# Three stacked graph-attention layers on one core: the extremes read two count tiles later, and first maxima two ahead on two accumulators

## The chip, the core and the metric

One NeuronCore of a Trainium2 chip runs the whole program. The metric is the device time of one execution in microseconds. The engines are named as in the profile: PE is TensorE, PEld its weight loads, DVE VectorE, ACT ScalarE, POOL GpSimd, and SP the engine that issues most of the DMAs.

## The reference

`x` has 3125 nodes of 128 features, and 103125 edges `src -> dst` are sorted by `dst`. Three attention layers run in two residual blocks:

```python
h = jnp.maximum(_layernorm(x, axis=-1), 0.0)
x = x + _L0_gnn_ref(h, ...)     # two layers, 128 -> 256 -> 128 features
h = jnp.maximum(_layernorm(x, axis=-1), 0.0)
x = x + _L1_gnn_ref(h, ...)     # one layer, 128 -> 128

def gat_layer(x, src, dst, W, a_src, a_dst, b, n_nodes):
    h = x @ W
    s, d = h @ a_src, h @ a_dst
    e = leaky_relu(s[src] + d[dst], 0.2)
    ex = exp(e - segment_max(e, dst)[dst])
    alpha = ex / segment_sum(ex, dst)[dst]
    return segment_sum(alpha[:, None] * h[src], dst) + b
```

(Each layer adds one loop per node to the edges. `edge_feat` is computed and never used.)

## The kernel before

**Dense form.** The edges are turned once into a table of counts `C`, kept in SBUF as 8-bit floats: for each pair of nodes, how many edges join them. Each layer then works on the dense 3125 x 3125 matrix. It is cut into 15 chunks `q` (3 layers x 5 chunks of 625 destinations), and each chunk into 25 source tiles `s` of 125 sources. I call the layers 0, 1, 2; chunks 0 to 4, 5 to 9 and 10 to 14 are theirs. Chunks 5 and 10 open a layer ("turn").

**Count stage.** 40 count tiles `t`. For each, VectorE makes two one-hot planes (L951), TensorE multiplies them (L1780), ScalarE copies the counts to `C` (L1452). Between the tiles other work is placed by tile number: after tile `EXT_AT` VectorE takes each partition's extremes of the attention terms (L968 to L980). SP writes them to DRAM and reads them back spread over all partitions. After tile `OVER_AT` VectorE reduces what came back (L997) and makes some scalars, and at tile `EXPS_AT` ScalarE makes exponentials from them. Then a row `g` goes through DRAM, and GpSimd makes the blocks of chunk 0 (L743, L751). TensorE multiplies these during count tiles `EARLY_AT` to 35.

**A chunk.** For a source tile `s`, `slot[s]` receives a block of 125 x 625 weights. It is either made by VectorE alone in one operation (`product`, L1149, from a row of exponentials that TensorE spreads over the partitions in PSUM) or by ScalarE (L1567, L1569) and GpSimd (L751) together. TensorE multiplies it by the features: 5 matmuls (L1813) a tile, in order of `s`, the last two tiles by L1821. Eight slots go round as a ring. I write P0, P1, P10, P24 for VectorE's product of tile 0, 1, 10, 24. Layer 1 has VectorE products at 0, 1, 2, 4, 8, 10, 14, 16, 20, 24, layer 2 the same without 0, and a turn chunk at 0, 1, 2, 4, 6, 8, 10, 12, 14, 16, 18, 24.

**First maxima.** Before the sums of chunk `q` can be scaled, the largest term of each destination is needed. VectorE runs 25 steps k0 to k24 over it (`next_top`, `top_step`, L1067; a first step of an accumulator is L1069), joins two accumulators `TOP0` and `TOP1` in PSUM (L1073), and TensorE transposes the result early in the next chunk (L1789), where VectorE reduces it (L1079, "the reduction" below). A step on an accumulator waits for the last step on the same one. The steps of chunk `q` stand between the products of chunk `q` at the places that `top_at(q, k)` gives. The first `AHEAD` of them come at the end of the chunk ahead, after its P24, and by `in_odd` all of these use `TOP0`:

```python
            return k >= AHEAD and k % 2 == 1     # in_odd: the step is on TOP1
```

**The rows.** TensorE spreads the row for chunk `q + 1` (`fast_rows`, L1803) after its tile 22 of chunk `q` (23 in a turn chunk), into the PSUM that the products of chunk `q` read. So it waits for P24 of chunk `q`, and nothing of chunk `q + 1` that reads it can start earlier:

```python
                dve.wait_ge(F.rows_ready, q)       # in product(q, s), and at s == 0 if that tile is GpSimd's
                pe.wait_ge(prod_done, prod_no(q, 0))   # in fast_rows(q)
```

The order on every engine is written out in the code; each engine runs its list in order, and semaphores join them.

Of the kernel before, what the change touches and what calls it, by code (L numbers as in the profile page):

```python
# [7 lines left out]
def gat_stack_kernel(nc, x, edges, apart, W1, a_src1, a_dst1, b1, W2, a_src2, a_dst2, b2,  # L8
# [11 lines left out]
    T = N // P  # L20
# [46 lines left out]
    with ctx:  # L67
# [290 lines left out]

        LAYERS = 3
        Q = LAYERS * NC  # L360
        AHEAD = 5
        PASS_AHEAD = 6
        EARLY_TILES = 15
        LATE = 20
# [2 lines left out]

        KEYS_TILE = 4
        FEAT_AT = tuple(KEYS_TILE + 2 + r for r in range(len(FEATS)))
        EXT_AT = FEAT_AT[-1] + 2  # L370
        OVER_AT = EXT_AT + 1
        EXPS_AT = OVER_AT + 1
        SECOND = 0
        EARLY_AT, EARLY_TO = EXPS_AT + 4, NT - 4
# [38 lines left out]
        def turn(q):  # L413
            return q and q % NC == 0

        def spread_tops(q, k0, k1, s0, s1):
            return tuple((s0 + (k - k0) * (s1 - s0) // (k1 - k0), q, k) for k in range(k0, k1))

        AFTER = T
        FIRST_TOPS = (None,  # L420
                      spread_tops(0, AHEAD, T, 0, 13) + spread_tops(1, 0, 10, 14, 25) + spread_tops(1, 10, 14, AFTER, AFTER),
                      spread_tops(1, 14, T, 0, 10) + spread_tops(2, 0, 17, 10, 25) + spread_tops(2, 17, 21, AFTER, AFTER),
                      spread_tops(2, 21, T, 0, 4) + spread_tops(3, 0, T, 4, 24) + spread_tops(4, 0, AHEAD, AFTER, AFTER))

# [18 lines left out]
        def in_odd(k, q=None):  # L443
            if q in (1, 2):
                return k % 2 == 1 and not any(at_ == AFTER and (c, k) == (q, k_) for at_, c, k_ in FIRST_TOPS[q])
            return k >= AHEAD and k % 2 == 1

# [8 lines left out]
        def top_at(q, k):  # L456
            if turn(q) and k >= LATE:
                return (21, 21, 22, 22, 23)[k - LATE]
            return (k - AHEAD) * (T - 3) // (T - 1 - AHEAD)

        def join_at(q):
            return top_at(q, T - 1) if turn(q) else top_at(q, T - 1) + 1
# [407 lines left out]
        def _(dve):  # L870
# [69 lines left out]
            def one_hots(t, part=None):  # L940
                c, i = t // JT, t % 2
                first, last_w = SPLIT[t % JT], SPLIT[t % JT + 1]
                w0, w1_ = 0, last_w - first
                if part is not None:
                    w0, w1_ = HALF[part][0], min(HALF[part][1], w1_)
                if t > 1 and w0 == 0:
                    dve.wait_ge(half_ok[1], t - 1)
                for n, (hot, key, m) in enumerate(((hot_lo[i], key_lo, COLS), (hot_col[i], key_col, P))):
                    if t % JT == 0:
                        dve.wait_ge(keys_sb, 2 * c + n + 1)  # L950
                    last = v.tensor_tensor(hot[:, w0:w1_, :, :],  # L951
                                           key[:, c, first + w0:first + w1_, :].unsqueeze(2).broadcast_to(
                                               [128, w1_ - w0, m, LANES]),
                                           iota_ps[:, 0:m, :].unsqueeze(1).broadcast_to([128, w1_ - w0, m, LANES]),
                                           ALU.is_equal)
                last.then_inc(hots_ok, 1)
# [14 lines left out]
            def extremes_early(L):  # L971
                if L:
                    dve.wait_ge(F.new_sb, (L - 1) * NC + EARLY_TILES // CT)
                    dve.wait_ge(ext_out, 16 * (2 * L - 1))
                else:
                    dve.wait_ge(ab_ready, len(FEATS))
                t1 = EARLY_TILES if L else T
                extremes(L, 0, t1)
                dve.wait_ge(ext_lin, EXT_NO[L])
                v.tensor_reduce(ext[:, 1:2], a_neg[:, 0:t1], AX.X, ALU.max).then_inc(ext_ready, 1)  # L980
# [14 lines left out]
            def over_nodes(e, into, done):  # L995
                dve.wait_ge(ext_in, 16 * (e + 1))
                v.tensor_reduce(into[:, :], ext_rows.rearrange("p (n i) -> p i n", i=2), AX.X, ALU.max).then_inc(done, 1)  # L997
# [44 lines left out]
            for t in range(KEYS_TILE + 1, NT - 1):  # L1042
                one_hots(t)
                if t == EXT_AT:
                    extremes_early(0)
                if t == OVER_AT:
                    over_nodes(0, extg[0], extg_ready)
# [105 lines left out]
            def next_top(q, k):  # L1153
                L = q // NC
                if turn(q) and k in (0, EARLY_TILES, LATE):
                    dve.wait_ge(unit_ready, 3 * L - 1 + (0, EARLY_TILES, LATE).index(k))
                top_step(F, a_unit[L % 2], q, k)
# [8 lines left out]
            def chunk(q):  # L1166
                L, c = q // NC, q % NC
                for s in range(T):
# [4 lines left out]
                    if q < len(FIRST_TOPS):  # L1173
                        first_tops(q, s)
                    else:
                        for k in range(AHEAD, T):
                            if top_at(q, k) == s:
                                next_top(q, k)
                        if s == join_at(q):
                            join_tops(F, q)  # L1180
# [33 lines left out]
                elif q < Q - 1:  # L1214
                    for k in range(AHEAD):
                        next_top(q + 1, k)
# [826 lines left out]
```

## Time and profile before

| | us |
|---|---|
| median of 3 runs | 687.71 (687.67 to 689.26) |
| the profiled execution | 687.7 |
| its span, first to last instruction | 686.0 |
| VectorE busy | 639.8 (93%) |
| TensorE busy | 587.9 (86%) |
| ScalarE busy | 484.7 (71%) |
| GpSimd busy | 459.6 (67%) |

The span is 1.7 us shorter than the execution's own time. A busy share is an average over the count stage (to about 204 us) and the chunks.

### The profile page before, as it was taken

The page shows a single profiled execution, that of the slowest core. Times are in us where ns is not written, and L with a number is a line of the kernel's source. Part 1 is how long each engine was busy: PE and PEld are TensorE (multiplying, and loading weights), DVE is VectorE, ACT ScalarE, POOL GpSimd, SP SyncE. Part 2 cuts the span into 40 slices and gives each one's busy share as a digit, 9 for nine tenths or more (in the row PEclk, how much of TensorE's full clock was granted, in tenths as well). Part 3 has the DMA queues.
Part 4 walks back from the last instruction along what each step waited for, and adds up shares of the span by engine and source line. Part 5 has one row for each costly group of instructions (what it writes and reads, how often), then busy time and mean ns, then how long its engine had stood idle before and what let it go on. Part 6 is the DMA issues. An engine that isn't in the chain of part 4 may idle for free.

```text
span 686.0 us, 13824 instructions
## 1 busy us (share of the span) xinstructions
PE 587.9 (86%) x5571; PEld 570.1 (83%) x5571; DVE 639.8 (93%) x911; ACT 484.7 (71%) x719; POOL 459.6 (67%) x448
## 2 busy tenths in 40 slices
PE   1728845989869899999999979999989989999995
PEld 1628744988769899989999979899989979999994
DVE  3999979999999989999987999999998899999994
ACT  0416543655969787887765878989886698898891
POOL 5579103589908656675954775858598688697883
PEclk9959977899999899999999999999999999999998
DMA  2410002000000000000100100000010010110001
GB/s 69 119 56 2 1 9 38 1 2 1 20 1 1 20 1 20 1 1 9 20 20 1 27 1 20 1 19 2 8 20 20 1 27 3 37 29 11 20 1 42
DMA packets 22325, 12.07 MB, mean 18 GB/s; under 512 B 12393, under 2 KB 20055, under 8 KB 22255
## 3 DMA queue, kind: packets, MB, share of 16 engines
q1 hardware_dynamic: 21455, 9.85, 6.2%
q0 software_dynamic: 800, 1.26, 0.6%
q8 instruction: 46, 0.75, 0.5%
q14 instruction: 24, 0.20, 0.1%
HBM read 9.47 MB, written 1.64 MB: 16 GB/s over the span
## 4 chain that ended last, share of the span: by engine, by line
DVE 52%; PE 28%; issue 8%; DMA 6%; POOL 4%; ACT 1%; POOLq 0%; DVEq 0%; SPq 0%
PE ps L1813 21%; DVE scratch L951 21%; DVE ps L1067 16%; DVE scratch L1149 5%; DMA xr<-in_x 3%; POOL scratch L751 2%; DVE ps L1069 2%; DVE ps L1079 1%; PE ps L1866 1%; PE ps L1821 1%; DMA gathered<-ext_lines 1%; PE ps L1844 1%; DVE scratch L1067 1%; DMA gathered<-in_edges,start_i 1%; DMA ext_lines<-ext 1%
## 5 line engine op out<-in xcount | busy, mean ns | idle before, releaser
L1813 PE MATMUL ps<-hB,scratch 125*125 125x129 f32 x3450 | 404.7, 276 | 21.3 <-DVE scratch L1149 17.8
L1813 PEld LDWEIGHTS ps<-hB,scratch 125*125 125x125 f32 x3450 | 390.7, 189 | 28.6 <-DVE scratch L1149 23.0
L751 POOL TENSOR_TENSOR scratch<-scratch,C 125x625 f32<-125x625 f32 x239 | 304.1, 1283 | 124.1 <-ACT scratch L1569 122.1
L1067 DVE SCALAR_TENSOR_TENSOR ps<-C,a_unit,ps 125x625 f32<-125x625 fp8e3 x330 | 275.5, 867 | 2.3
L1567 ACT ACTIVATE scratch<-gathered,r_neg 125x625 f32<-125x625 f32 x219 | 176.6, 806 | 18.7 <-PE ps L1813 17.5
L1569 ACT ACTIVATE scratch<-scratch,r_src 125x625 f32<-125x625 f32 x219 | 179.0, 817 | 7.1
L1452 ACT ACTIVATE C<-ps 125x1000 fp8e3<-125x1000 f32 x80 | 78.0, 1000 | 78.5 <-PE ps L1780 78.3
L1780 PE MATMUL ps<-scratch 128*128 128x125 bf16 x1250 | 90.3, 235 | 40.0 <-DVE scratch L951 38.1
L1780 PEld LDWEIGHTS ps<-scratch 128*128 128x128 bf16 x1250 | 83.0, 105 | 46.8 <-DVE scratch L951 44.7
L1149 DVE SCALAR_TENSOR_TENSOR scratch<-ps,r_src,C 125x625 f32<-125x625 f32 x121 | 104.2, 861 | 4.2 <-PE ps L1803 4.1
L951 DVE TENSOR_TENSOR scratch<-key_lo,ps 128x4096 bf16<-128x4096 bf16 (+3 forms) x41 | 89.8, 2190 | 0.0
L951 DVE TENSOR_TENSOR scratch<-key_col,ps 128x4000 bf16<-128x4000 bf16 (+3 forms) x41 | 87.9, 2144 | 0.0
L1069 DVE TENSOR_SCALAR ps<-C,a_unit 125x625 f32<-125x625 fp8e3 x30 | 25.8, 865 | 0.2
L756 POOL TENSOR_TENSOR scratch<-scratch,rz 125x640 f32<-125x640 f32 x14 | 17.6, 1258 | 11.8 <-DVE rz L1126 11.8
L743 POOL TENSOR_SCALAR scratch<-gathered,r_src 125x625 f32<-125x625 f32 x20 | 15.7, 783 | 10.7 <-DMA gathered<-g_lines 10.7
L1550 ACT ACTIVATE kappa<-back 125x5 f32<-125x5 f32 x15 | 3.1, 207 | 27.0 <-DVE back L1093 26.9
L1821 PE MATMUL ps<-hB,scratch 125*125 125x129 f32 x150 | 21.6, 274 | 0.0
L1821 PE MATMUL ps<-hB,gathered 125*125 125x129 f32 x150 | 21.4, 273 | 0.0
L728 POOL TENSOR_TENSOR shift<-sigma,tau 125x1 f32<-125x1 f32 x3 | 0.6, 192 | 30.7 <-DVE tau L1013 30.7
L1079 DVE TENSOR_REDUCE ps<-ps 125x5 f32<-125x625 f32 x15 | 12.2, 812 | 8.2 <-PE ps L1789 8.2
L790 POOL TENSOR_TENSOR hB<-hA,e_src 125x645 f32<-125x645 f32 x15 | 19.0, 1265 | 0.0
L1821 PEld LDWEIGHTS ps<-hB,scratch 125*125 125x125 f32 x150 | 18.8, 187 | 0.2 <-POOL scratch L751 0.2
(195 smaller groups left out, 451.5 us busy)
## 6 DMA issues: line engine op xcount, KB each, us to landing
gathered<-g_lines SPq DMA_DIRECT2D x15, 305.2 KB
xr<-in_x SPq DMA_DIRECT2D x1, 1562.5 KB
out<-xr SPq DMA_DIRECT2D x4, 312.5 KB
edge_sb<-in_edges SPq DMA_DIRECT2D x1, 805.7 KB
gathered<-ext_lines SPq DMA_DIRECT2D x5, 122.1 KB
w<-in_W SPq DMA_DIRECT2D x2, 128.0 KB
out<-xr SPq DMA_DIRECT2D x1, 187.5 KB
out<-xr SPq DMA_DIRECT2D x1, 125.0 KB
```

The source lines that it names most:

```text
L751: g.tensor_tensor(slot[s], slot[s], C5[:, q % NC, s, :], ALU.mult).then_inc(pool_done, 1)
L951: last = v.tensor_tensor(hot[:, w0:w1_, :, :], key[:, c, first + w0:first + w1_, :].unsqueeze(2).broadcast_to([128, w1_ - w0, m, LANES]), ...
L1067: v.scalar_tensor_tensor(dest, counts, unit[:, s:s + 1], top, ALU.min, ALU.max).then_inc(S.top_done, 1)
L1069: v.tensor_scalar(dest, counts, unit[:, s:s + 1], None, ALU.min).then_inc(S.top_done, 1)
L1079: v.tensor_reduce(mu[:, :], tiles(WORK), AX.X, ALU.max).then_inc(S.top_max, 1)
L1149: v.scalar_tensor_tensor(slot[s].rearrange("p (t n) -> p t n", n=P), tiles(ROWU), r_src[L % 2][:, s:s + 1], C5[:, c, s, :].rearrange("p (t ...
L1452: a_.activation(C5[:, c, :, rows].rearrange("p t (w q) -> p t w q", q=WQ), tiles(place(t, i), w1_ - w0).rearrange("p w (t q) -> p t w q", ...
L1567: a_.activation(A, ga[q % 2], ACT.Relu, bias=r_neg[L % 2][:, s:s + 1]).then_inc(over_done, 1)
L1569: a_.activation(A, A, ACT.Identity, bias=r_src[L % 2][:, s:s + 1]).then_inc(rowmax_ok, 1)
L1780: last = mm(ps[0:128, o:o + WC], hot_lo[i][:, w, :, k], hot_col[i][:, w, :, k], start=(k == 0), stop=(k == KC - 1))
L1813: last = mm(ps[0:P, acc_at(t):acc_at(t) + HW], A[:, P * t:P * (t + 1)], feat, start=opens and t in (0, 3), stop=closes, skip_group_check=True)
L1821: last = mm(ps[0:P, acc_at(t):acc_at(t) + HW], slot[s][:, P * t:P * (t + 1)], hB3[:, s, :], start=False, stop=s == T - 1, skip_group_check ...
```

## The change

Three constants and one formula. `AHEAD` falls from 5 to 2; `top_at` spreads the other 23 steps over places 0 to 21, where 20 steps stood at 0 to 22; `EXT_AT` goes from 14 to 15 and `OVER_AT` from 15 to 17. `EXPS_AT` (16 to 18) and `EARLY_AT` (20 to 22) follow from `OVER_AT`.

```diff
-        AHEAD = 5
+        AHEAD = 2
@@
-        EXT_AT = FEAT_AT[-1] + 2
-        OVER_AT = EXT_AT + 1
+        EXT_AT = FEAT_AT[-1] + 3
+        OVER_AT = EXT_AT + 2
         EXPS_AT = OVER_AT + 1
         SECOND = 0
         EARLY_AT, EARLY_TO = EXPS_AT + 4, NT - 4
@@
-            return (k - AHEAD) * (T - 3) // (T - 1 - AHEAD)
+            return (k - AHEAD) * (T - 4) // (T - 1 - AHEAD)
```

Worked out (T is 25): before, k5 to k24 stand at places 0, 1, 2, 3, 4, 5, 6, 8, 9, 10, 11, 12, 13, 15, 16, 17, 18, 19, 20, 22. Now k2 and k3 stand at 0, then k4 at 1, k5 at 2, and so on to k23 at 20 and k24 at 21. The work of no engine changes in amount.

The first place is VectorE in the count stage, around the extremes (L968 to L980) and what is read back (L997). The rows with + and - are those that moved.

```order
 L951 TENSOR_TENSOR scratch<-key_col,ps 128x4000
+L951 TENSOR_TENSOR scratch<-key_lo,ps 128x3328
+L951 TENSOR_TENSOR scratch<-key_col,ps 128x3250
 L968 TENSOR_SCALAR a_neg<-ab 125x25
 L969 TENSOR_REDUCE ext<-ab 125x1
 L980 TENSOR_REDUCE ext<-a_neg 125x1
-L951 TENSOR_TENSOR scratch<-key_lo,ps 128x3328
-L951 TENSOR_TENSOR scratch<-key_col,ps 128x3250
+L951 TENSOR_TENSOR scratch<-key_lo,ps 128x4096
+L951 TENSOR_TENSOR scratch<-key_col,ps 128x4000
+L951 TENSOR_TENSOR scratch<-key_lo,ps 128x4096
+L951 TENSOR_TENSOR scratch<-key_col,ps 128x4000
 L997 TENSOR_REDUCE extg<-gathered 125x2
```

One count tile (two L951) stood between the extremes and the reading back, and now there are two, both full ones.

The second place is VectorE at the border of chunks 6 and 7 (layer 1), from P24 to the reduction L1079 of the chunk ahead. Before:

```order
L1149 SCALAR_TENSOR_TENSOR gathered<-ps,r_src,C 125x625
L1069 TENSOR_SCALAR ps<-C,a_unit 125x625
L1067 SCALAR_TENSOR_TENSOR ps<-C,a_unit,ps 125x625 x4
L1149 SCALAR_TENSOR_TENSOR scratch<-ps,r_src,C 125x625
L1069 TENSOR_SCALAR ps<-C,a_unit 125x625
L1149 SCALAR_TENSOR_TENSOR scratch<-ps,r_src,C 125x625
L1067 SCALAR_TENSOR_TENSOR ps<-C,a_unit,ps 125x625
L1149 SCALAR_TENSOR_TENSOR scratch<-ps,r_src,C 125x625
L1067 SCALAR_TENSOR_TENSOR ps<-C,a_unit,ps 125x625
L1079 TENSOR_REDUCE ps<-ps 125x5
```

Now, at the same border:

```order
L1149 SCALAR_TENSOR_TENSOR gathered<-ps,r_src,C 125x625
L1069 TENSOR_SCALAR ps<-C,a_unit 125x625
L1067 SCALAR_TENSOR_TENSOR ps<-C,a_unit,ps 125x625
L1149 SCALAR_TENSOR_TENSOR scratch<-ps,r_src,C 125x625
L1067 SCALAR_TENSOR_TENSOR ps<-C,a_unit,ps 125x625
L1069 TENSOR_SCALAR ps<-C,a_unit 125x625
L1149 SCALAR_TENSOR_TENSOR scratch<-ps,r_src,C 125x625
L1067 SCALAR_TENSOR_TENSOR ps<-C,a_unit,ps 125x625
L1149 SCALAR_TENSOR_TENSOR scratch<-ps,r_src,C 125x625
L1067 SCALAR_TENSOR_TENSOR ps<-C,a_unit,ps 125x625
L1079 TENSOR_REDUCE ps<-ps 125x5
```

P24 and P0 (the first two L1149) have two steps between them in place of five; between P0 and the reduction there are four steps in place of three.

The third place is VectorE at the border of chunks 11 and 12 (layer 2, where tile 0 is GpSimd's), from P24 to P1. Before:

```order
L1149 SCALAR_TENSOR_TENSOR gathered<-ps,r_src,C 125x625
L1069 TENSOR_SCALAR ps<-C,a_unit 125x625
L1067 SCALAR_TENSOR_TENSOR ps<-C,a_unit,ps 125x625 x4
L1069 TENSOR_SCALAR ps<-C,a_unit 125x625
L1149 SCALAR_TENSOR_TENSOR scratch<-ps,r_src,C 125x625
```

Now:

```order
L1149 SCALAR_TENSOR_TENSOR gathered<-ps,r_src,C 125x625
L1069 TENSOR_SCALAR ps<-C,a_unit 125x625
L1067 SCALAR_TENSOR_TENSOR ps<-C,a_unit,ps 125x625 x2
L1069 TENSOR_SCALAR ps<-C,a_unit 125x625
L1149 SCALAR_TENSOR_TENSOR scratch<-ps,r_src,C 125x625
```

Four steps stand between P24 and P1 in place of six. The wait for the rows (at `s == 0`) stood before the sixth step; it now stands before the third.

## Rows read from the trace of the kernel before

**Rows 1.** Busy time in a stretch of layer 2, each engine's us and count

```profile
583.00:612.00 29.00, 28.82 (x261) 28.61 (x261) 28.79 (x45) 25.51 (x36) 23.41 (x19) 1.00 0.08 23
```

**Rows 2.** VectorE in order of time, count stage: start us, us, operation, idle before

```profile
92.71 0.18 DVE L980 TENSOR_REDUCE ext<-a_neg 125x1 f32<-125x25 f32 x1
...
99.83 0.41 DVE L997 TENSOR_REDUCE extg<-gathered 125x2 f32<-125x250 f32 x1 [3.39 <-DMA gathered<-ext_lines]
...
101.15 2.28 DVE L951 TENSOR_TENSOR scratch<-key_lo,ps 128x4096 bf16<-128x4096 bf16 x1
...
105.50 2.28 DVE L951 TENSOR_TENSOR scratch<-key_lo,ps 128x4096 bf16<-128x4096 bf16 x1
```

**Rows 3.** ScalarE in order of time, count stage

```profile
101.27 0.32 ACT L1476 ACTIVATE g_row<-b_cut,sigma 125x25 f32<-125x25 f32 x1 [2.01 <-DVE tau L1013]
```

**Rows 4.** GpSimd in order of time, first and last block of chunk 0

```profile
114.85 0.79 POOL L743 TENSOR_SCALAR scratch<-gathered,r_src 125x625 f32<-125x625 f32 x1 [10.74 <-DMA gathered<-g_lines]
...
178.23 1.31 POOL L751 TENSOR_TENSOR gathered<-gathered,C 125x625 f32<-125x625 f32 x1
```

**Rows 5.** TensorE in order of time, where chunk 0 ends

```profile
188.56 0.87 PE L1821 MATMUL ps<-hB,scratch 125*125 125x129 f32 x6
```

**Rows 6.** VectorE in order of time, chunks 6 to 7, layer 1

```profile
416.51 0.87 DVE L1149 SCALAR_TENSOR_TENSOR gathered<-ps,r_src,C 125x625 f32<-125x625 f32 x1
...
418.19 3.60 DVE L1067 SCALAR_TENSOR_TENSOR ps<-C,a_unit,ps 125x625 f32<-125x625 fp8e3 x4
421.82 0.87 DVE L1149 SCALAR_TENSOR_TENSOR scratch<-ps,r_src,C 125x625 f32<-125x625 f32 x1
...
426.79 0.82 DVE L1079 TENSOR_REDUCE ps<-ps 125x5 f32<-125x625 f32 x1 [0.22 <-PE ps L1789]
...
436.40 0.84 DVE L1149 SCALAR_TENSOR_TENSOR scratch<-ps,r_src,C 125x625 f32<-125x625 f32 x1
437.15 3.19 DVE L1067 SCALAR_TENSOR_TENSOR ps<-C,a_unit,ps 125x625 f32<-125x625 fp8e3 x4
```

**Rows 7.** TensorE in order of time, chunks 6 to 7

```profile
421.01 0.71 PE L1803 MATMUL ps<-ident,g_row 125*125 125x125 f32 x5
...
429.86 6.87 PE L1813 MATMUL ps<-hB,scratch 125*125 125x129 f32 x60 [0.90 <-DVE scratch L1149]
437.29 6.87 PE L1813 MATMUL ps<-hB,scratch 125*125 125x129 f32 x60 [0.56 <-DVE scratch L1149]
...
453.36 0.71 PE L1803 MATMUL ps<-ident,g_row 125*125 125x125 f32 x5
```

**Rows 8.** TensorE in order of time, chunks 5, 9 and 10

```profile
361.55 2.47 PE L1813 MATMUL ps<-hB,scratch 125*125 125x129 f32 x20 [0.50 <-DVE scratch L1149]
...
509.60 1.36 PE L1813 MATMUL ps<-hB,scratch 125*125 125x129 f32 x10 [0.92 <-POOL scratch L751]
...
537.65 4.80 PE L1813 MATMUL ps<-hB,scratch 125*125 125x129 f32 x40 [0.64 <-DVE scratch L1149]
```

**Rows 9.** VectorE in order of time, P0 of chunk 5

```profile
350.21 0.87 DVE L1149 SCALAR_TENSOR_TENSOR scratch<-ps,r_src,C 125x625 f32<-125x625 f32 x1 [2.57 <-PE ps L1803]
```

**Rows 10.** P0 of chunk 6 on VectorE

```profile
387.33 0.87 DVE L1149 SCALAR_TENSOR_TENSOR scratch<-ps,r_src,C 125x625 f32<-125x625 f32 x1
```

**Rows 11.** TensorE's rows for chunk 6

```profile
385.37 0.71 PE L1803 MATMUL ps<-ident,g_row 125*125 125x125 f32 x5
```

**Rows 12.** TensorE in order of time, chunks 11 and 12, layer 2

```profile
565.66 19.54 PE L1813 MATMUL ps<-hB,scratch 125*125 125x129 f32 x175 [0.72 <-DVE scratch L1149]
...
586.68 0.71 PE L1803 MATMUL ps<-ident,g_row 125*125 125x125 f32 x5
...
594.82 21.19 PE L1813 MATMUL ps<-hB,scratch 125*125 125x129 f32 x190 [0.18 <-DVE scratch L1149]
```

**Rows 13.** VectorE in order of time, the sixth step (k5) of chunk 12

```profile
588.54 0.87 DVE L1069 TENSOR_SCALAR ps<-C,a_unit 125x625 f32<-125x625 fp8e3 x1
```

**Rows 14.** Who waited for whom, whole span: us in total, times, longest

```profile
PE ps L1813 <- DVE scratch L1149: 17.8, 24, 3.6
DVE scratch L1149 <- PE ps L1803: 4.1, 2, 2.6
```

## The prediction

> **What bounds the kernel now.** I read the table of waits first, then the engines side by side in order of time. The waits [rows 14] show TensorE and VectorE waiting for each other: TensorE 17.8 us in 24 places for products, VectorE 4.1 us in 2 places for the spread rows. Neither is the bound alone: in layer 2 both are busy for 28.8 of 29 us [rows 1]. The count stage is VectorE's: its one-hots stand end to end, 4.35 us a full tile (105.50 less 101.15), and it stops once, 3.39 us, for the extremes that come back through DRAM [rows 2].
>
> In the chunks the order of time shows a loop. Take chunk 7, layer 1. TensorE spreads the rows at 421.01 and is done at 421.72. P0 starts at 421.82, 0.10 later [rows 6, 7]. The four steps ahead of it start at 418.19 and end at 421.79, so their starts are 0.91 apart, and the next operation could have started at about 421.7 [rows 6]. So P0 waits for the rows, just barely, and the five steps ahead are what fills the time. From P0 VectorE runs to P10 (436.40, done 437.24); TensorE waits for P10 (0.56 us) and starts at 437.29. From there it has no wait until the next rows at 453.36 [rows 6, 7]. The loop is rows, P0, P10, TensorE, rows: 453.36 - 421.01 = 32.35 us. What stands between P0 and P10 costs its time in every turn of it. What stands between P24 and P0 costs nothing, as long as it ends before the rows do. Chunk 5 shows that more plainly: its P0 waits 2.57 us for the rows [rows 9].
>
> **The change part by part.**
>
> *The extremes.* They were done at 92.89 and their reduction could start at 99.83, so the trip takes 6.9 us [rows 2]. Now two full tiles, 8.7 us, lie over it: the wait of 3.39 is gone, with 1.8 us to spare. What is late next is the start of chunk 0's blocks. The scalars come two tiles less 3.39 later, 5.3 us, and ScalarE now has to empty count tile 17 before its exponentials, which it did not have to wait for at 101.27 [rows 3]; I put `g` 7 us later, at most 8.7. GpSimd then starts at about 122 in place of 114.85. Its last block was done at 179.54 and TensorE took it at 188.56, 9.0 us later [rows 4, 5]; TensorE now comes 3.4 earlier, and 9.0 - 3.4 = 5.6 is less than 7. But GpSimd stood idle for ScalarE's four blocks in that stretch, and this idle time shrinks when it starts late, since they stay tied to count tiles. I take it as hidden. If not, it costs up to 8.7 - 5.6 = 3.1 us. **-3.4 us.**
>
> *The alternation.* Steps on one accumulator start 0.91 us apart, alternating ones (3.19 - 0.87) / 3 = 0.77 apart [rows 6]. So each step that no longer follows one on its own accumulator saves 0.13 us. That counts only where VectorE is not waiting behind it: at the start of chunk 1, where k0 to k24 stand in one run and TensorE waits for their end, it is 2 x 0.13. **-0.3 us.** The Trainium skill ("VectorE: DVE Perf Modes", section "The DRAIN you can't avoid") says that the next operation doesn't start until the pipe is empty, and that a semaphore between them costs nothing. By that both spacings would be equal and this term zero, the sum 0.3 higher; the rows show 0.77 against 0.91, and I go by them.
>
> *Layer 1, chunks 7 and 8.* Between P24 and P0 there are now 2 steps. VectorE is ready for P0 at about 419.1 and waits 2.7 us for the rows, which are no earlier. From P0 to P10 (places 0 to 9) stood k5 to k13, 9 steps; now k2 to k12, 11 steps. Two more at 0.77 are 1.55. The reduction between them waited 0.22 us for TensorE's transposes [rows 6], which one more step ahead of it swallows: +1.3. TensorE's wait for P10 goes from 0.56 to about 1.3 (and that for P4, 0.90 now, to 1.4 [rows 7]); nothing behind P10 has room to give it back, since TensorE then runs without a wait. P14 has the same two steps more and P16 to P24 three, but TensorE takes 1.1 us a tile (6.87 us for six [rows 7]) and comes to them later and later. **+2.6 us for both.** Bounds: 0 (if VectorE's lead were kept) and 2 x 1.55 = 3.1.
>
> *Layer 1, the others.* Chunk 6: P0 was not held by the rows; it started at 387.33, the rows were done at 386.08 [rows 10, 11]. Now it can start at 386.18, 1.15 earlier, and P10 comes 1.55 - 1.15 = 0.4 later, or 0.6 with a wait at the reduction. **+0.6.** Chunk 9: P10 is 1.5 late, but TensorE then waits 0.92 us for GpSimd's tile 15 [rows 8], whose work hangs on VectorE's scalars at place 4, one step late. **+0.8.**
>
> *The turns.* Chunk 5: P0 is held by the rows before and after [rows 9]. The last wait of TensorE for VectorE is at 361.55, for P6 [rows 8]: k2 to k8 stand ahead of it in place of k5 to k10, one more. **+0.8.** Chunk 10: the last one is at 537.65, for P10 [rows 8], with 11 steps in place of 9. **+1.55.** Chunk 4 opens in the same way but TensorE is behind VectorE there; between 0 and one step, I take **+0.2.** Chunks 0 to 3 keep their order but for single steps.
>
> *Layer 2.* The wait for the rows now stands ahead of k2. The rows of chunk 12 are done at 587.39 and k5 started at 588.54 [rows 12, 13], 1.05 after it could have. Now k2 starts at 587.5, k3 0.77 later, P1 at 589.0 where it was 588.54 + 0.77 = 589.3. So the first products are 0.3 earlier here, P10 and P14 one step (0.77) later than they, and TensorE's wait of 0.18 for P4 goes [rows 12]. At P10 it comes back in part. In chunk 11 a wait of 0.72 shrinks in the same way. Bounds: 0 and 0.72 + 3 x 0.18 = 1.3 gained. The low end is nearer, as P10 takes over. **-0.4 us.**
>
> The sum: -3.4 - 0.3 + 2.6 + 0.6 + 0.8 + 0.8 + 1.55 + 0.2 - 0.4 = +2.45 us. The profiled execution took 687.7 us, its span 686.0, and the median of the runs is 687.71, so the same sum holds for both: **690.1 us**.
>
> **The rivals.**
>
> *Half of it.* Somewhere the extra steps meet time that VectorE or TensorE would have waited anyway: the 0.22 wait at the reduction is one such place, and the 0.92 wait for GpSimd another. If each loop lost only one step (0.77) in chunks 5 to 10, they would cost 4.6 in place of 6.35, and with the gain of layer 2 at its upper end the time is 687.7 - 3.7 + 4.6 + 0.2 - 1.3 = 687.5; with one of the two, 688.2. For it: VectorE's list holds many small operations that wait for their own results. Against it: P0 starts 0.10 us after the rows, as close as a release can follow.
>
> *Faster: the loop is not held at the rows.* The mechanism is that P0 can come earlier with two steps ahead than with five. If TensorE reaches its tile 22 earlier than now, because P4 and P10 were its only waits, then P0 moves up and VectorE's 0.1 us a step of alternation adds up. That needs the rows at least 1.3 us earlier a chunk in layer 1; from there on nothing is lost, and the time is 687.7 - 3.7 = 684.0, less with layer 2. For it: in chunk 6 P0 does move up by 1.15 us. Against it: the rows come after tile 22 in TensorE's list, and TensorE works without a pause from 437.29 to 453.36 [rows 7].
>
> *Slower still.* VectorE's steps at place 3 also feed the factor that ScalarE needs before its further blocks, and these go to GpSimd and on to TensorE. If ScalarE's chain is then the later one, the loops lose 1.55 each where I take 0.6 to 0.8, in chunks 5, 6 and 9 (+2.5), or GpSimd comes late in the count stage (+3.1): about 692.5.
>
> **How the numbers follow.** The forecast as worked out 0.52, half of it 0.23, faster 0.13, slower still 0.12. The forecast's own range is 689.0 to 691.2. For eight in ten I leave out the faster case and part of the slowest: 686.9 to 692.2. A run here can tell about 0.3% (2.06 us) from no change, so the borders are 685.65 and 689.77. The forecast lies above the upper one, but close: of its 0.52 I put 0.33 above and 0.19 inside; half of it falls inside; so slower 0.45, same 0.42, faster 0.13.
>
> **What the profile after would show.** L997 in the count stage without an idle time, and what follows it 3.4 us earlier. VectorE waiting 2 to 3 us for L1803 ahead of each P0 of chunks 4 to 10, several times the 4.1 that stand now [rows 14], and TensorE's waits for L1149 near 1.3 us at P4 and P10. Rows of layer 1 33.65 us apart in place of 32.35; layer 2 chunks at 29.0 to 29.1. If P0 in layer 1 has no wait, the loop is not what I say. If the rows are 32.3 us apart although P0 waits, TensorE's wait at P10 was not on it. If TensorE waits for GpSimd in the 130 to 190 us of the count stage, the first term is too good.

## The result, and the profile after

| | before | after |
|---|---|---|
| median, us | 687.71 (687.63 to 689.26, 5 runs) | 691.26 (690.71 to 691.95, 5 runs) |
| span of the profiled execution | 686.0 | 689.3 |

The ratio is 1.0047, with a 95% interval of 1.0033 to 1.0062: the changed kernel is slower by 3.5 us. The forecast was 690.1 us, range 686.9 to 692.2; 691.26 lies 0.06 us outside the narrow range of the forecast as worked out (689.0 to 691.2).

The count stage first. VectorE in order of time (start us, us, operation, idle before in brackets), the rows that answer to [rows 2]:

```profile
96.10 0.18 DVE L980 TENSOR_REDUCE ext<-a_neg 125x1 f32<-125x25 f32 x1
...
104.88 0.41 DVE L997 TENSOR_REDUCE extg<-gathered 125x2 f32<-125x250 f32 x1
```

L997 has no idle time left. ScalarE's `g`, GpSimd's first and last block of chunk 0, and TensorE at the end of chunk 0, which answer to [rows 3 to 5]:

```profile
108.52 0.30 ACT L1476 ACTIVATE g_row<-b_cut,sigma 125x25 f32<-125x25 f32 x1
...
121.66 0.79 POOL L743 TENSOR_SCALAR scratch<-gathered,r_src 125x625 f32<-125x625 f32 x1 [11.03 <-DMA gathered<-g_lines]
...
178.92 1.31 POOL L751 TENSOR_TENSOR gathered<-gathered,C 125x625 f32<-125x625 f32 x1
...
184.91 0.87 PE L1821 MATMUL ps<-hB,scratch 125*125 125x129 f32 x6
```

`g` is 7.25 us later (108.52 less 101.27) and GpSimd starts 6.8 later, but its last block is only 0.7 later and TensorE still takes it 3.65 us earlier than before. So GpSimd's idle time swallowed the delay.

The loop of layer 1, chunks 6 to 7, VectorE from P24 to P10 and TensorE from rows to rows (answering to [rows 6, 7]):

```profile
412.55 0.87 DVE L1149 SCALAR_TENSOR_TENSOR gathered<-ps,r_src,C 125x625 f32<-125x625 f32 x1
413.33 0.86 DVE L1069 TENSOR_SCALAR ps<-C,a_unit 125x625 f32<-125x625 fp8e3 x1
414.23 0.87 DVE L1067 SCALAR_TENSOR_TENSOR ps<-C,a_unit,ps 125x625 f32<-125x625 fp8e3 x1
417.56 0.87 DVE L1149 SCALAR_TENSOR_TENSOR scratch<-ps,r_src,C 125x625 f32<-125x625 f32 x1 [2.46 <-PE ps L1803]
...
422.99 0.81 DVE L1079 TENSOR_REDUCE ps<-ps 125x5 f32<-125x625 f32 x1
...
433.37 0.84 DVE L1149 SCALAR_TENSOR_TENSOR scratch<-ps,r_src,C 125x625 f32<-125x625 f32 x1
```

```profile
416.74 0.71 PE L1803 MATMUL ps<-ident,g_row 125*125 125x125 f32 x5
...
426.05 6.93 PE L1813 MATMUL ps<-hB,scratch 125*125 125x129 f32 x60 [1.13 <-DVE scratch L1149]
434.26 6.87 PE L1813 MATMUL ps<-hB,scratch 125*125 125x129 f32 x60 [1.29 <-DVE scratch L1149]
...
450.33 0.71 PE L1803 MATMUL ps<-ident,g_row 125*125 125x125 f32 x5
```

P0 waits 2.46 us for the rows, from P0 to P10 it is 15.81 us where it was 14.58, the reduction has lost its wait, and the rows are 33.59 us apart (450.33 less 416.74) where they were 32.35. In chunk 5, P0 waits 3.48 us ([rows 9]: 2.57); in chunk 6 it now waits too, 1.48 us, where it was not held ([rows 10, 11]).

TensorE's waits in chunk 5 and chunk 10 (answering to [rows 8]), and both engines in layer 2 ([rows 12, 13]):

```profile
357.47 2.47 PE L1813 MATMUL ps<-hB,scratch 125*125 125x129 f32 x20 [0.50 <-DVE scratch L1149]
...
538.16 2.03 PE L1813 MATMUL ps<-hB,scratch 125*125 125x129 f32 x16 [1.29 <-DVE scratch L1149]
...
587.59 0.71 PE L1803 MATMUL ps<-ident,g_row 125*125 125x125 f32 x5
...
602.98 14.58 PE L1813 MATMUL ps<-hB,scratch 125*125 125x129 f32 x130 [0.72 <-DVE scratch L1149]
```

```profile
588.33 0.87 DVE L1067 SCALAR_TENSOR_TENSOR ps<-C,a_unit,ps 125x625 f32<-125x625 fp8e3 x1 [0.19 <-PE ps L1803]
```

In layer 2, k2 does start right after the rows, as forecast, but TensorE now waits 0.72 us for P10, where it had no wait for it. And the table of waits, whole span (us in total, times, longest; [rows 14]), with the busy times from 583 to 612 us, same columns as [rows 1]:

```profile
PE ps L1813 <- DVE scratch L1149: 22.6, 23, 2.5
...
DVE scratch L1149 <- PE ps L1803: 15.5, 7, 3.5
```

```profile
583.00:612.00 29.00, 28.28 (x255) 28.03 (x254) 28.70 (x44) 25.16 (x35) 22.78 (x19) 1.00 0.08 24
```

TensorE is busy 0.54 us less in the same 29 us: that is the new wait.

**Where the 3.3 us of the span lie.** I compare the starts of the rows L1803 of each chunk. "Chunk 7" is the time from the rows for chunk 7 to the rows for chunk 8. Chunk 0 lies in the first line; chunks 2 and 3 differ by 0.01 and are left out.

| part | before | after | difference | forecast |
|---|---|---|---|---|
| to the rows for chunk 1 | 204.24 | 200.60 | -3.64 | -3.4 |
| chunk 1 | 34.02 | 32.71 | -1.31 | -0.3 |
| chunk 4 | 35.02 | 35.11 | +0.09 | +0.2 |
| chunk 5 | 36.00 | 36.77 | +0.77 | +0.8 |
| chunk 6 | 35.64 | 35.46 | -0.18 | +0.6 |
| chunks 7, 8 | 64.69 | 67.17 | +2.48 | +2.6 |
| chunk 9 | 34.46 | 35.20 | +0.74 | +0.8 |
| chunk 10 | 35.64 | 37.19 | +1.55 | +1.55 |
| chunks 11 to 14, to the end | 130.20 | 133.00 | +2.80 | -0.4 |

One pair of profiles carries these differences, and the same program varies between profiled executions: in the nine profiles with the changed kernel's count stage the rows for chunk 1 stand at 200.60 to 203.72 us, and the changed kernel's own is the earliest of them. So the first line may not be read to 0.1 us; the times of whole runs below carry it.

Three lines are off: chunk 1, chunk 6 and layer 2. The experiments go after these, and after the loop itself.

### The profile page after: what moved, and what is told of

It reads as the page before. It is cut to its first block, busy times and chain, and to the rows that moved or that the text cites. A ratio compares the mean times of both kernels' runs of the same rounds, so it can differ in the third digit from the quotient of the medians.

```text
span 689.3 us, 13825 instructions
## 1 busy us (share of the span) xinstructions
PE 593.0 (86%) x5571; PEld 573.9 (83%) x5571; DVE 639.6 (93%) x911; ACT 485.8 (70%) x719; POOL 459.6 (67%) x448
## 4 chain that ended last, share of the span: by engine, by line
DVE 43%; PE 37%; issue 8%; DMA 5%; POOL 4%; ACT 2%; POOLq 0%; DVEq 0%
PE ps L1813 29%; DVE scratch L951 20%; DVE ps L1067 10%; DVE scratch L1149 5%; DMA xr<-in_x 3%; POOL scratch L751 2%; PE ps L1866 2%; DVE ps L1079 1%; PE ps L1844 1%; PE ps L1803 1%; PE ps L1836 1%; PE ps L1869 1%; DMA gathered<-in_edges,start_i 1%; ACT scratch L1567 1%; PE ps L1780 1%
## 5 line engine op out<-in xcount | busy, mean ns | idle before, releaser
L1780 PE MATMUL ps<-scratch 128*128 128x125 bf16 x1250 | 93.3, 239 | 32.7 <-DVE scratch L951 30.8
L1780 PEld LDWEIGHTS ps<-scratch 128*128 128x128 bf16 x1250 | 85.7, 108 | 40.0 <-DVE scratch L951 37.9
L1149 DVE SCALAR_TENSOR_TENSOR scratch<-ps,r_src,C 125x625 f32<-125x625 f32 x121 | 104.2, 861 | 15.5 <-PE ps L1803 15.5
L951 DVE TENSOR_TENSOR scratch<-key_lo,ps 128x4096 bf16<-128x4096 bf16 (+3 forms) x41 | 89.3, 2179 | 0.0
L951 DVE TENSOR_TENSOR scratch<-key_col,ps 128x4000 bf16<-128x4000 bf16 (+3 forms) x41 | 87.4, 2132 | 0.0
L756 POOL TENSOR_TENSOR scratch<-scratch,rz 125x640 f32<-125x640 f32 x14 | 17.6, 1257 | 16.7 <-DVE rz L1126 16.7
L1821 PEld LDWEIGHTS ps<-hB,gathered 125*125 125x125 f32 x150 | 18.8, 188 | 0.0
```

The costliest lines, as they stand in the source:

```text
L951: last = v.tensor_tensor(hot[:, w0:w1_, :, :], key[:, c, first + w0:first + w1_, :].unsqueeze(2).broadcast_to([128, w1_ - w0, m, LANES]), ...
L1149: v.scalar_tensor_tensor(slot[s].rearrange("p (t n) -> p t n", n=P), tiles(ROWU), r_src[L % 2][:, s:s + 1], C5[:, c, s, :].rearrange("p (t ...
L1780: last = mm(ps[0:128, o:o + WC], hot_lo[i][:, w, :, k], hot_col[i][:, w, :, k], start=(k == 0), stop=(k == KC - 1))
L1821: last = mm(ps[0:P, acc_at(t):acc_at(t) + HW], slot[s][:, P * t:P * (t + 1)], hB3[:, s, :], start=False, stop=s == T - 1, skip_group_check ...
```

## The experiments

My theory of the loss was the loop of the prediction: a step between P0 and P10 costs its time in every turn. The rival to it: what is lost is the lead of three steps over a chunk's border, wherever they are put. For layer 2 the theory at hand was the extra step, or a collision with GpSimd (below). Each run has the kernel before beside it on the same chip; the ratio is to that.

### The two halves apart

```diff
 # e1_extremes_only: before, with
+        EXT_AT = FEAT_AT[-1] + 3
+        OVER_AT = EXT_AT + 2
 # e2_two_ahead_only: before, with
+        AHEAD = 2
+            return (k - AHEAD) * (T - 4) // (T - 1 - AHEAD)
```

> The kernel before with the extremes' part alone (EXT_AT 15, OVER_AT 17); AHEAD stays 5. My theory: the chunks keep their periods of before, and all is earlier by what the count stage gained, 3.6 us at chunk 1's first maxima: 684.1 us. Whether the further 1.3 us that chunk 1 gained in the changed kernel comes with this part (its ScalarE and GpSimd work is placed by count tile) is open: then 682.8 us. Rival: the gain is given back where later work waits for something that did not move; then 686 us or more.

> The kernel before with AHEAD 2 and the new top_at alone; the extremes stay where they were. If the two parts add up, 691.3 + 3.6 = 694.9 us, or 691.3 + 5.0 = 696.3 us if all of chunk 1's gain comes with the extremes' part. In any case the rows of chunks 5 to 14 keep the distances of the changed kernel (33.6 us in chunks 7 and 8, 29.8 in layer 2). Rival: the loss in layer 2 comes from where the count stage's shift put GpSimd against VectorE; then layer 2 stays at 29.2 us a chunk and the time is 2.8 us less.

Measured: the extremes alone 684.52 us against 688.28, ratio 0.9948 (0.9934 to 0.9961). Two ahead alone 694.89 us, ratio 1.0101 (1.0085 to 1.0116). That is -3.8 and +6.6 us, +2.8 together, against +3.5 for both in one kernel; by the ratios it is -0.52% and +1.01%, +0.49% together, against +0.47%. So the parts add up, and the gain of the extremes is kept to the end: the first run has chunks 7, 8, 12 and 13 at 32.36, 32.34, 29.17 and 29.17 us, as before. The second has them at 33.57, 33.57, 29.81 and 29.87, as after. The rival that layer 2's loss comes from the shift of the count stage falls.

Chunk 1 took 32.86 us in the first run and 32.71 in the second, so its 1.3 us seemed to come with both parts. Most of it comes with neither. Busy time of TensorE in single microseconds of chunk 1, the number behind it the granted clock, before:

```profile
226.00:227.00 1.00, 1.00 (x5) 0.50 0.00 0
...
231.00:232.00 1.00, 1.00 (x8) 0.55 0.00 0
232.00:233.00 1.00, 1.00 (x12) 1.00 0.12 48
```

and after:

```profile
224.00:225.00 1.00, 1.00 (x7) 0.50 0.00 0
225.00:226.00 1.00, 1.00 (x7) 0.61 0.00 0
226.00:227.00 1.00, 1.00 (x11) 1.00 0.00 0
```

After the waits at the border of chunk 1 (2.24 and 0.86 us before) TensorE runs at a granted clock of 0.50, that is 1.2 GHz, 5 to 8 matmuls in a microsecond in place of 11 or 12. Before, this lasts from about 225.1 to 231.9 us, after from 222.4 to 225.8. In the two halves it is short as well (3.4 us), although the first has the chunk's steps as before. The other way round, the run with the old steps in layer 2 alone (e4_five_ahead_in_layer_2, below) has the changed kernel's chunk 1 and the long stretch, and takes 33.47 us there. So about 1.1 of the 1.31 us are a difference of clock between two profiled executions, and 0.15 to 0.2 belong to the alternation (32.71 against 32.86; the join L1073 stands at 223.18 in the second run, 223.37 before). The same stretch of 1.2 GHz appears in chunk 6 near 394 us in some profiles and not in others: the first run took 36.88 us there, before 35.64, with the same program in that chunk.

### Reading back later, without later extremes

```diff
 # e10_read_back_only: before, with
-        OVER_AT = EXT_AT + 1
+        OVER_AT = EXT_AT + 2
```

> The kernel before with OVER_AT two tiles behind EXT_AT, but EXT_AT left at 14: of the first run's edit only the later reading back. The trip through DRAM took 6.9 us; between the extremes and L997 now stand a short tile and a full one, 3.5 + 4.35 = 7.9 us, so the wait of 3.39 us goes as well and the gain is the first run's, 3.4 to 3.8 us below before. Rival: the later extremes matter too (they let ScalarE and SP start the trip undisturbed); then the wait stays in part and the gain is under 2.5 us.

Measured: 685.69 us against 689.66, ratio 0.9944 (0.9930 to 0.9958). VectorE, the extremes and the reading back:

```profile
92.46 0.18 DVE L980 TENSOR_REDUCE ext<-a_neg 125x1 f32<-125x25 f32 x1
...
100.45 0.41 DVE L997 TENSOR_REDUCE extg<-gathered 125x2 f32<-125x250 f32 x1
```

No wait is left, and the ratio agrees with the first run's. The gain is that of the second tile over the trip; that the extremes are made a tile later gives nothing.

### Where the steps stand

```diff
 # e3_steps_behind_P10: after, with
-            return (k - AHEAD) * (T - 4) // (T - 1 - AHEAD)
+            return (0, 1, 2, 3, 4, 5, 6, 8, 9, 10, 10, 11, 12, 13, 14, 15, 16, 17, 17, 18, 19, 20, 21)[k - AHEAD]
```

> The changed kernel with another spread of the steps: AHEAD 2 and the accumulators stay, but only nine steps stand at places 0 to 9, as before, and fourteen at 10 to 21. My theory (the loop rows, P0, P10, TensorE, rows): chunks 5 and 7 to 10 get back what they lost, 0.8 + 1.2 + 1.2 + 0.7 + 1.55 = 5.5 us, and so does layer 2 (2.8 us), since P10 there comes no later than before: 691.3 - 8.3 = 683.0 us, with chunks 7 and 8 at 32.35 us. Rival: what is lost is the lead of three steps, wherever they are put, because P14 to P24 then come late in place of P10: then chunks 7 and 8 stay above 33 us and the time at 690 to 691 us. In between: layer 1 recovers and layer 2, where VectorE is busy all the time, does not: 685.8 us.

Measured: 682.64 us, ratio 0.9908 (0.9893 to 0.9923). The lead over the border is two steps, as in the changed kernel, and nearly everything lost is back: chunk 5 takes 36.00 us, chunk 9 34.48, chunks 12 and 13 28.86 and 28.96. The rival of the lead falls. Four chunks stay above before: 7 and 8 at 32.59 and 32.60 us (before 32.35), chunk 10 at 36.40 (before 35.64), and chunk 6 at 36.66 (before 35.64), where this profile has 6.8 us at 1.2 GHz and before has none. (The profiled execution was the slowest of this kernel, 686.75 us.) TensorE, chunk 7, from P4 on:

```profile
428.95 6.87 PE L1813 MATMUL ps<-hB,scratch 125*125 125x129 f32 x60 [0.90 <-DVE scratch L1149]
436.38 7.12 PE L1813 MATMUL ps<-hB,scratch 125*125 125x129 f32 x60 [0.56 <-DVE scratch L1149]
```

The waits for P4 and P10 are those of before to 0.01 us [rows 7]. The stretch behind P10 is 7.12 us where it was 6.87, and VectorE has five steps between P10 and P14 in place of four: P14 is late by 0.25. Chunk 10 shows the same one tile on: three steps stand between P10 and P12 in place of two, P12 starts 19.67 us after the start of the rows where it was 18.90, and TensorE now waits 0.64 us for it. The reading of P14, and five steps ahead in the turns, were tried next.

```diff
 # e7_turns_five_ahead: e3's kernel, with
+        def ahead(q):                      # used in in_odd, top_at and both loops over the steps
+            return 5 if q and turn(q) else AHEAD
+            if turn(q):
+                return (k - 5) * (T - 3) // (T - 1 - 5)
+            return (0, 1, 2, 3, 4, 5, 6, 8, 9, 10, 11, 12, 13, 14, 15, 16, 17, 17, 18, 19, 20, 21, 22)[k - AHEAD]
 # e8_eight_ahead_of_P10: the same with
+            return (0, 1, 2, 3, 4, 6, 8, 9, 10, 10, 11, 12, 13, 14, 15, 16, 17, 17, 18, 19, 20, 21, 22)[k - AHEAD]
```

> The third run's kernel (nine steps at places 0 to 9) mended in two places: chunks 5 and 10 take five steps ahead and the places of before, and in the other chunks only four steps stand at 10 to 13 and ten at 14 to 22. The third run had 36.40 us in chunk 10 (before: 35.64) and 32.59 us in chunks 7 and 8 (before: 32.35). My theory: chunk 10 falls to 35.6, and chunks 7 and 8 to 32.35, since P14 is no longer late; layer 2 stays at 28.9: 682.0 - 0.8 - 0.5 = 680.7 us by the lower runs, 681.4 us by the median. Rival: the 0.24 us of chunks 7 and 8 come from elsewhere (the scalars at place 9, or ScalarE), and the time stays within 0.5 us of the third run's.

> The same as the run ahead of this one, but with eight steps at places 0 to 9 in place of nine, and five at 10 to 13. In chunks 7 and 8 TensorE still waited 0.90 us for P4 and 0.56 for P10 with nine. My theory (each step between P0 and P10 costs its 0.77 in each loop, as long as TensorE waits for P10): P10 comes 0.77 earlier and TensorE's wait of 0.56 goes, so chunks 7 and 8 take 31.8 us in place of 32.35, and the time is 1 to 2 us less than with nine. Rival: VectorE's own work fills the loop (31.7 to 31.9 us of 32.6 in the third run), so that the step only comes back behind P10, at P14 to P24, and the chunks stay at 32.3 us.

Measured with nine: 680.94 us against 688.93, ratio 0.9888 (0.9872 to 0.9903). Chunks 7 and 8 take 32.35 and 32.34 us: the late P14 was the 0.25. Chunk 10 stays at 36.34, so that part of the expectation was wrong. The trace says why: with five steps ahead P0 of chunk 10 has no wait for the rows any more and starts 1.57 us after the start of the rows, where before, and in the third run (e3_steps_behind_P10), it was 0.84. That is 0.73 of lateness for 0.70 us in the chunk.

With eight: 683.91 us, ratio 0.9927 (0.9913 to 0.9940), 3 us more than with nine where I expected 1 to 2 less. Yet the point of the run came out: chunks 7 and 8 take 31.93 and 31.93 us, 0.42 less, and TensorE has no wait left at P10:

```profile
427.55 13.78 PE L1818 MATMUL ps<-hB,scratch 125*125 125x129 f32 x120 [0.90 <-DVE scratch L1154]
```

(Line numbers are 5 higher here.) One step is worth 0.77, and the wait for P10 was 0.56, so not more than about that could be won. The rest is lost at P14: the list has five steps between P10 and P14 again, P14 is done at 438.81 us, and TensorE runs 5 matmuls from 438.5 to 439.0 where it runs 7 in each half microsecond before. From eleven steps to nine a step was worth 0.62 us in these chunks (33.59 against 32.35), from nine to eight 0.42. Ten were not run. What came back elsewhere, in the profiles: chunk 5 takes 36.83 us in place of 36.00, chunk 10 37.61 in place of 36.34, and chunk 12 29.04 in place of 28.72. In the turns this kernel has five steps ahead of P0, and there P0 shows no wait for the rows, it is late itself: it starts 1.68 us after the start of the rows in chunk 5 and 2.83 in chunk 10 (before 0.84 in both). VectorE has no spare time left there, and the five steps that were free before are now on the path. Two more differences of these profiles I do not put down to the edit: 1.3 us in the count stage, which is the same program, and 1.24 in chunk 6, where only this one has a stretch of 1.2 GHz (the next run has this chunk's steps, no such stretch, and takes 33.67 us against 35.34 here).

```diff
 # e9_two_lists: after, with
+            if NC < q < 2 * NC:
+                return (the list with eight)[k - AHEAD]
+            return (the list with nine)[k - AHEAD]
```

> AHEAD 2 in all chunks as in the changed kernel, with eight steps at places 0 to 9 in chunks 6 to 9 (the list of the run before this one) and nine in the others; the turns' steps follow the same list up to k19. My theory: chunks 7 and 8 take 31.9 us as in the run with eight; chunks 5 and 10 take 36.0 and about 36.4 us, as in the third run, since with two steps ahead VectorE is not late for P0 when the chunks ahead of a turn are quicker; layer 2 stays at 28.7 to 29.0: 0.8 us less than with nine everywhere (680.9), so 680.1 us. Rival: VectorE has no slack left, and what chunks 7 and 8 gain comes back in chunk 10 (37.6 us there in the run with eight); then 681.5 us or more.

Measured: 680.01 us against 689.66, ratio 0.9868 (0.9853 to 0.9883). Chunks 5, 7, 8 and 10 take 36.00, 31.92, 31.93 and 35.73 us, chunks 12 and 13 28.73 and 28.95. With two steps ahead everywhere P0 of chunk 10 starts 0.84 us after the start of the rows again and the turns are not hurt. Chunk 10 is better than I expected, since this list has two steps between P10 and P12, the third run's three. This is the fastest version: 1.3% under before and, by the two ratios, 1.8% under the changed kernel. Of the 1.3%, the later reading back alone gives 0.5 to 0.6 (0.9948 and 0.9944 above) of it; the rest comes with the steps.

### Layer 2

```diff
 # e4_five_ahead_in_layer_2: after, with AHEAD and top_at of before in chunks 11 to 14
+        def ahead(q):
+            return 5 if q is not None and q > 2 * NC else AHEAD
 # e5_scale_a_place_earlier: after, with the layer's place of L1113, in USUAL[2]
-                 At(1, (3, 4, 5, 6), 6, (8, 9, 10), None, (14, 17, 20), (None,) * 3, (None,) * 3, None, None))
+                 At(1, (3, 4, 5, 6), 6, (7, 9, 10), None, (14, 17, 20), (None,) * 3, (None,) * 3, None, None))
```

> The changed kernel, but chunks 11 to 14 with five steps ahead and the places of before. If the loss of layer 2 comes from its own steps, chunks 12 to 14 return to 29.2 us and the time is 691.3 - 2.8 = 688.5 us. Rival: the loss comes from how VectorE's small operations fall against GpSimd's (L1113 took 0.90 us in place of 0.16), by chance of phase: then only part returns, between 689 and 691 us, and L1113 still takes 0.9 us.

> The changed kernel with one constant different: in layer 2 the first operation on the sums (L1113, the scale) stands at place 7 in place of 8, in USUAL[2].z; no step is moved. My theory: in the changed kernel this operation falls on one of GpSimd's blocks and takes 0.90 us in place of 0.16, and holds P10 back by that in each of chunks 11 to 14. At place 7 it would start near 598.64, while GpSimd is idle from 598.57 to 599.82: it takes 0.16 us, P10 comes 0.7 earlier, TensorE's wait of 0.7 to 0.8 us for it goes, and the time falls by up to 4 x 0.7 = 2.8 us, to 688.5 us, with chunks 12 and 13 at 29.2 us. Rival: the loss is the one step more ahead of P10 alone, and the operation's 0.9 us is only time that VectorE would have stood in anyway; then 691.3 us and 29.8 us a chunk.

Measured with the old steps: 689.24 us, ratio 1.0009 (1.0000 to 1.0018); chunks 11 to 13 take 30.90, 29.16 and 29.17 us, those of before to 0.02. In chunks 1 to 10 the places are the changed kernel's. So layer 2's loss comes with its own steps. But in this run L1113 takes 0.17 us again as well, so it doesn't say whether the steps or L1113 is the cause.

Measured with the steps of the changed kernel and only the small operation L1113 moved: 689.10 us, ratio 1.0002 (0.9993 to 1.0011), and chunks 11 to 13 take 30.54, 29.07 and 29.07 us, less than before. The same steps stand between the rows and P10. L1113 is what was in the way. VectorE and GpSimd in the changed kernel, chunk 12:

```profile
598.64 0.86 DVE L1149 SCALAR_TENSOR_TENSOR scratch<-ps,r_src,C 125x625 f32<-125x625 f32 x1
599.42 0.86 DVE L1067 SCALAR_TENSOR_TENSOR ps<-C,a_unit,ps 125x625 f32<-125x625 fp8e3 x1
600.19 0.90 DVE L1113 TENSOR_TENSOR ps<-scratch,kappa 125x5 f32<-125x5 f32 x1
601.01 0.86 DVE L1067 SCALAR_TENSOR_TENSOR ps<-C,a_unit,ps 125x625 f32<-125x625 fp8e3 x1
```

```profile
599.82 1.25 POOL L751 TENSOR_TENSOR scratch<-scratch,C 125x625 f32<-125x625 f32 x1 [1.26 <-ACT scratch L1569]
```

L1113 works on 125x5 elements. It starts while GpSimd's block runs and ends at 601.09; the block ends at 601.07. In the run with it moved it falls into GpSimd's idle time:

```profile
599.17 0.17 DVE L1113 TENSOR_TENSOR ps<-scratch,kappa 125x5 f32<-125x5 f32 x1
```

```profile
597.86 1.25 POOL L751 TENSOR_TENSOR scratch<-scratch,C 125x625 f32<-125x625 f32 x1 [0.40 <-ACT scratch L1569]
600.37 1.24 POOL L751 TENSOR_TENSOR scratch<-scratch,C 125x625 f32<-125x625 f32 x1 [1.26 <-ACT scratch L1569]
```

Over the span the 14 of them take 2.3 us before and in this run, and 5.4 us after: 0.73 to 0.80 more in each of chunks 11 to 14. So the new steps without the collision cost nothing; what they did is move L1113 onto a block. The collision without the new steps was in no run.

The same collision stands in chunk 6, there in the kernel before. VectorE's L1020, one element, and the GpSimd block that it falls on, before:

```profile
393.49 1.20 DVE L1020 SCALAR_TENSOR_TENSOR counts_fit<-ext_all,covers 1x1 f32<-1x1 f32 x1
```

```profile
393.44 1.25 POOL L751 TENSOR_TENSOR scratch<-scratch,C 125x625 f32<-125x625 f32 x1 [0.31 <-ACT scratch L1569]
```

and after:

```profile
389.04 0.15 DVE L1020 SCALAR_TENSOR_TENSOR counts_fit<-ext_all,covers 1x1 f32<-1x1 f32 x1
```

```profile
387.80 1.25 POOL L751 TENSOR_TENSOR scratch<-scratch,C 125x625 f32<-125x625 f32 x1 [0.31 <-ACT scratch L1569]
389.36 1.24 POOL L751 TENSOR_TENSOR scratch<-scratch,C 125x625 f32<-125x625 f32 x1 [0.31 <-ACT scratch L1569]
```

After, it fits between two blocks (389.05 to 389.36), and chunk 6 has won 1.05 us by accident: TensorE's wait for P4 behind it falls from 3.61 to 2.55 us. It is so in every profile with either list: L1020 takes 1.20 or 1.21 us in the three with the old steps in chunk 6, 0.15 in the five with the changed kernel's. No run moves L1020 alone.

### The alternation

```diff
 # e6_alternation_off: after, with
-            return k >= AHEAD and k % 2 == 1
+            return k >= 5 and k % 2 == 1
```

> The changed kernel with in_odd at k >= 5: k2, k3 and k4 go to TOP0 again, all places stay. By the spacings of the trace (0.91 on one accumulator, 0.77 on alternating ones) k3 starts 0.13 later behind k2, once in each of chunks 4 to 14 and three times in chunk 0, on the way from the rows to P10: at most 11 x 0.13 + 0.4 = 1.8 us, so 691.3 to 693.1 us, and I take 692.5. Rival: the alternation is worth more, since it is what lets VectorE reach P10 at all; then 694 us or more.

Measured: 693.18 us against 688.93, ratio 1.0064 (1.0050 to 1.0077). By the medians that is 1.9 us above the changed kernel, by the two ratios 1.2 us, and the intervals of the ratios overlap, so the time alone doesn't settle it. The profiles do: chunks 5 to 13 are each 0.09 to 0.14 us longer than after, the 0.13 of one spacing; chunk 1 is 0.23 longer. The rival falls. Chunk 4 is 0.53 us longer, but it varied by 0.2 (35.08 to 35.31) between other runs with the same steps, so that part says little.

## Why the prediction came out as it did

The time was met within 1.2 us (690.1 against 691.26), and the terms that rest on the loop were right. But the sum was off by so little because errors took each other away: +3.2 in layer 2, -1.0 in chunk 1 and -0.8 in chunk 6. That the number came out this close is in part luck.

**The extremes, -3.4.** Right: -3.8 us measured alone, and -3.64 in the pair of profiles (with the caution above). That the late start of GpSimd is hidden was right as well: its last block came 0.7 us late where I had allowed 5.6. The "slower still" rival had its +3.1 there.

**The alternation, -0.3.** Right in kind: 0.15 to 0.2 at the border of chunk 1. It was counted there alone. The run without it shows 0.13 in each later chunk too, but those lie inside the terms of the chunks, where I reckoned every step at 0.77. By the two sentences that the prediction took from the Trainium skill ("VectorE: DVE Perf Modes", section "The DRAIN you can't avoid"), turning the alternation off would have changed nothing; the run shows 0.09 to 0.14 us a chunk. But the prediction had read only part of that section: it also says that a next operation that is not held starts earlier, so it doesn't make the two spacings equal. Its sentence that a semaphore costs nothing does not fit the 0.91 us of these rows against 0.77. The rest of chunk 1's -1.31 was clock, of which the prediction had nothing.

**Layer 1, chunks 7 to 9, and the turns.** Right to 0.1 us a chunk: 1.24 and 1.24 for 1.3, 0.74 for 0.8, 0.77 for 0.8, 1.55 for 1.55. TensorE's wait for P10 is 1.29 us, forecast about 1.3; the rows 33.59 us apart, forecast 33.65. The runs with nine and eight steps ahead of P10 show the cause: same lead, same accumulators, other places, and the time is back.

**Chunk 6, +0.6.** The step of the loop was right: a run with this chunk's steps as in the changed kernel and no stretch of 1.2 GHz in it took 35.00 us (e4_five_ahead_in_layer_2). With L1020's 1.05 us taken off, before would be 34.59, and the difference +0.4. The profile after has such a stretch, before has none, and that is the other 0.46 (35.46 less 35.00). What failed is that I took all work between P0 and P4 at its length of before. L1020 stood in the trace with 1.20 us for one element, and I passed over it.

**Layer 2, -0.4.** This step failed, with the wrong sign: +2.8. The prediction said that the first products come earlier, P10 one step later, and that "the low end is nearer, as P10 takes over"; it took the small operations between them at their old length. Worked out again from the rows, P10 starts 14.50 us after the rows (602.09 less 587.59) where it started 13.31 after: the first step behind the rows is 1.12 earlier, two steps more cost 1.55, and L1113 costs 0.74 more; the sum is +1.17. In the run that takes the last piece away (L1113 moved), layer 2 takes 129.81 us from the rows for chunk 11 to the end, 0.39 less than before, where the forecast was 0.4. That it agrees so closely is luck, as the 0.4 was a choice between bounds of 0 and 1.3; the steps were right in kind. The failure is again a small operation taken at its old length.

**The rival "half of it".** Its second time is a slip: with the loops halved and layer 2 at -0.4 the sum is 687.7 - 3.7 + 4.6 + 0.2 - 0.4 = 688.4 us; the 688.2 leaves out the 0.2 of chunk 4. It changes nothing in the argument.

The Trainium skill ("SBUF — State Buffer", section "SBUF: two separate sides") has the rule that I had not weighed. VectorE and GpSimd share a pair of ports as an exclusive lock, and a VectorE operation with two inputs in SBUF is fully blocked while a GpSimd operation that reads SBUF is under way. The traces agree: L1113 (both inputs in SBUF) and L1020 (the same) end within 0.02 us of GpSimd's block, or take 0.15 to 0.17 us beside none. L1117, which reads PSUM alone, takes 0.16 us at 601.79, in the midst of the next block. In chunks 11 to 14 L1113 starts 0.36 to 0.38 us after the block does, so the block had come first each time.

## What to carry to other kernels

In a loop of two engines, first find the link that closes it; steps moved off the stretch between two links cost nothing there, steps moved onto it cost 0.6 to 0.8 us each in every turn here, and steps taken off it give that back only as far as the wait at its end is long and no later product becomes late. So the place of a step in the list counts more than how many are done ahead: the same two steps ahead with another list of places are 1.3% faster than before. The number ahead counts where the engine has no spare time, as at P0 of the turns. And in a list of small operations beside a busy GpSimd, look for any that takes as long as a large one: its length hangs on the phase, and a shift by a microsecond can bring 0.75 us a turn or take it away.

## What the runs showed of the hardware

- A VectorE operation of 125x5 or 1x1 elements with both inputs in SBUF took 0.90 to 0.97 and 1.20 us beside a GpSimd block, with its end on the end of the block, and 0.15 to 0.17 us without. One input in SBUF is no safeguard: L1040, a TENSOR_SCALAR of 125x5 elements that reads SBUF alone, takes 0.80 us in chunk 10 of both kernels. Before, it ends at 531.52, 0.02 us behind GpSimd's operation L756. It stands between P4 and P6, and no run moves it.
- TensorE ran at 1.2 GHz behind waits in chunk 1 and chunk 6, and for how long differed between profiled executions: in chunk 1 6.8 us in two, 3.4 in eight and none in two; in chunk 6 none in four, 3.4 in seven and 6.8 in one. In chunk 6 that made 1.24 us for the same program (36.88 against 35.64). The wait ahead of it doesn't tell them apart: before, TensorE waited 3.61 us in chunk 6 and had no such stretch; after, it waited 2.55 us and had one. Why one execution has it and another not stays open, and so does whether it explains the 1.1 us between the lower and the higher runs of the kernel before.
